# Second attention products issued for two steps at once, and the last tile's chunks transposed by TensorE

## The reference, cut to what matters

```python
# layer 0
x = _layernorm(x + _L0_attn_ref(x, ...))   # 16 heads of 64, every query against all 4096 keys
x = _layernorm(x + _L0_ffn_ref(x, ...))    # rows quantized in blocks of 32, then x @ W.T
# layer 1
x = _layernorm(x + _L1_attn_ref(x, ...))   # 16 query heads, 2 key heads, a window of 256
x = _layernorm(x + _L1_ffn_ref(x, ...))    # sigmoid(xr Wr) * (relu(xk Wk)^2 Wv)

# the first attention
scores = jnp.einsum('bhts,bshd->bhts', q_, k_) * scale + const
attn = jax.nn.softmax(scores, axis=-1)
out = jnp.einsum('bhts,bshd->bthd', attn, v_).reshape(B, T, D)
return quat_linear(out, oW, ob)
```

## Time and profile before

| | us |
|---|---|
| time, median of 3 runs | 2162.46 (2153.24 to 2162.77) |
| the profiled execution | 2166.97 |
| span of its slowest core (3) | 2165.4 |
| spans of the 8 cores | 2133.8 to 2165.4 |
| busy in the span: PE, ACT, DVE, POOL | 1953.6, 1595.8, 1063.2, 406.3 |

### The profile page before, as it was taken

One profiled execution on the slowest core, in us unless ns is written; L12 is line 12 of the kernel. 1 busy time (PEld: TensorE's weight loads), 2 busy tenths in 40 slices (PEclk: granted clock), 3 DMA queues, 4 the chain that ended last, 5 costly groups with the idle time before them and its releaser, 6 DMA issues.

```text
span 2165.4 us, 42335 instructions; the slowest of 8 cores (2133.8 to 2165.4 us)
## 1 busy us (share of the span) xinstructions
PE 1953.6 (90%) x14234; PEld 783.8 (36%) x14234; DVE 1063.2 (49%) x1569; ACT 1595.8 (74%) x2177; POOL 406.3 (19%) x271
## 2 busy tenths in 40 slices
PE   5999998988999999899999999998790899999996
PEld 2444445322222222222222222222440356556653
DVE  6566542575321345423445224453680467777773
ACT  1343348999899999899999999998220577777772
POOL 3000000000010000100001000001010166776665
PEclk9999999999999999999999999999995999999998
DMA  6332311003210010010101104004219211111110
GB/s 98 78 64 54 49 33 46 26 23 92 73 59 6 4 45 26 27 57 6 42 21 33 59 1 90 16 16 117 68 41 112 60 31 41 41 41 50 40 41 40
DMA packets 63855, 100.99 MB, mean 47 GB/s; under 512 B 25617, under 2 KB 46225, under 8 KB 62242
## 3 DMA queue, kind: packets, MB, share of 16 engines
q1 hardware_dynamic: 41138, 67.77, 11.3%
q0 software_dynamic: 22512, 30.51, 8.4%
HBM read 88.86 MB, written 22.02 MB: 51 GB/s over the span
## 4 chain that ended last, share of the span: by engine, by line
PE 57%; ACT 22%; issue 9%; DVE 6%; DMA 4%; POOL 1%; ACTq 1%; DVEq 0%; POOLq 0%; SPq 0%
ACT TE L728 20%; PE PALL L1121 12%; PE PALL L1244 8%; PE PALL L1134 7%; PE PALL L1148 7%; PE PALL L1152 5%; PE PALL L1169 4%; PE PALL L1311 3%; PE PALL L1210 2%; PE PALL L1266 2%; PE PALL L1255 2%; DMA TY<-Y2SP 2%; PE PALL L1257 2%; PE PALL L1276 1%; DMA Y2SP<-TY 1%
## 5 line engine op out<-in xcount | busy, mean ns | idle before, releaser
L728 ACT ACTIVATE TE<-PALL,BIASB 128x1024 bf16<-128x1024 f32 x1088 | 1124.9, 1132 | 85.8 <-PE PALL L1134 76.4
L1134 PE MATMUL PALL<-TE,TY 64*128 64x512 bf16 (+1 forms) x2560 | 429.6, 353 | 73.6 <-ACT TE L728 48.3
L1148 PE MATMUL PALL<-TE,TY 128*64 128x512 bf16 (+1 forms) x2560 | 447.9, 373 | 0.4 <-ACT TE L728 0.4
L1152 PE MATMUL PALL<-TE,TY 128*64 128x512 bf16 x2176 | 423.9, 386 | 0.0
L1134 PEld LDWEIGHTS PALL<-TE,TY 64*128 64x128 bf16 x2560 | 131.4, 93 | 524.6 <-issue 522.5
L1148 PEld LDWEIGHTS PALL<-TE,TY 128*64 128x64 bf16 x2560 | 133.3, 110 | 236.4 <-issue 225.7
L994 DVE COPY TY<-PALL 128x512 f32<-128x512 f32 (+1 forms) x40 | 24.5, 612 | 358.2 <-PE PALL L1152 358.2
L743 ACT ACTIVATE TY<-PALL,SMALL 128x384 bf16<-128x384 f32 x272 | 156.9, 589 | 34.3 <-DVE SMALL L1029 32.4
L600 POOL TENSOR_TENSOR TX<-TX 128x1024 f32<-128x1024 f32 x17 | 40.0, 2354 | 724.2 <-DVE TY L924 724.2
L689 ACT ACTIVATE TX<-PALL,BIASB 128x512 f32<-128x512 f32 (+1 forms) x104 | 66.4, 661 | 141.9 <-PE PALL L1121 141.7
L1029 DVE TENSOR_REDUCE SMALL<-PALL 128x2 f32<-128x768 f32 x136 | 129.7, 954 | 76.1 <-PE PALL L1257 72.9
(11 more groups left out here) (130 smaller groups left out, 2296.4 us busy)
## 6 DMA issues: line engine op xcount, KB each, us to landing
TE<-WOD SPq DMA_DIRECT2D x5, 2048.0 KB, 8.4
TX<-XST SPq DMA_DIRECT2D x17, 512.0 KB, 4.6
TY<-Y2SP POOLq DMA_DIRECT2D x17, 512.0 KB, 3.5
YOUT<-TY SPq DMA_DIRECT2D x17, 512.0 KB, 2.6
TE<-FWD SPq DMA_DIRECT2D x4, 2048.0 KB, 8.3
Y2SP<-TY SPq DMA_DIRECT2D x17, 256.0 KB, 2.2
TE<-XF POOLq DMA_DIRECT2D x8, 512.0 KB, 11.9
TY<-XF POOLq DMA_DIRECT2D x8, 512.0 KB, 10.9
```

Source lines behind the costliest of these rows:

```text
L728: s.activation(EXPS(m), PB(2 * (m % 2), 0, 1024), AF.Exp, bias=BIASB[:, 63:64], scale=0.125).then_inc(*up("exp", m))
L1134: op = t.matmul(PB(2 * (m % 2) + hh, x * w, w), KB(c, (s * k + x) * 128, 128, 64 * hh, 64), QB(c, 0, w, 64 * hh, 64), start=True, stop=Tru ...
L1148: t.matmul(PB(6, 0, w)[64 * hh:64 * hh + 64, :], VB(s * k + x, (2 * c + hh) * 64, 64), EXPS(m)[:, hh * 512 + x * w:hh * 512 + x * w + w], ...
L1152: op = t.matmul(PB(7, 0, 512)[64 * hh:64 * hh + 64, :], ONEB, EXPS(m)[:, hh * 512:hh * 512 + 512], start=(s == 0), stop=(s == SPP[T] - 1), ...
```

## The change

**Attention.** `pv_plan` is gone. At every odd step `n` from 3 on TensorE issues `scores(n)` and then the second products of steps `n - 3` and `n - 2` together: first all products with values of both steps, then all with ones. The first of a group waits for the copy out of bank 6 (`pvn`) only, and the products with ones for that of bank 7 (`pvf`). Nothing is put off at a group's start. The pieces beside are moved to even steps: `o` every second step, `f` at b + 16, 18, 22, 24, 28, 30, 34, 36; `t`, `z2`, `n2` and the load of the next input move by two to five steps.

**Chunks.** `n2` of tiles 0 to 3 writes into `XD` and no longer into `XDT`. `tev` does not wait for the store any more; `n2` waits for the transposes of the next chunk, `quant` for the store of the chunk two before, and `xld` for the store instead of for `n2`.

**Passage.** The four chunks of the last tile are placed anew: the small tile's projections first, `z1` of all four before the first `quant`, `tev` on ScalarE. The last transposed DMA is gone: for each of the four chunks TensorE transposes the chunk (`yt`), ScalarE copies it into `X2` (`yte`), and the ten projections of the chunk follow with 128 columns. The load `wk` is issued right after the attention's last product, the third transposed DMA after the load of `f`'s weights instead of ahead of it.

```diff
-def pv_plan():
-
-
-    plan, due, last = {}, [], 0
-    for m, (T, c, s) in enumerate(STEPS):
-        last = max(last, m + (4 if s == 0 and m else 2))
-        due.append(last)
-    for m, n in enumerate(due):
-        plan.setdefault(n, []).append(m)
...
-            put("pe", o + d * i, "o", T, j, i)
+            put("pe", o + 2 * i, "o", T, j, i)
...
-        put("pe", b + 10, "t", T, j)
-        put("dve", b + 11, "tev", T, j)
-        for i in range(8):
-            put("pe", b + 13 + d2 * i, "f", T, j, i)
-        z = b + 13 + 7 * d2 + 2
-        put("dve", z, "z2", T, j)
-        put("act", z + 4, "r2", T, j)
-        put("dve", z + 6, "n2", T, j)
-        put("sp", z + 6, "y2", T, j)
+        put("pe", b + 12, "t", T, j)
+        put("dve", b + 13, "tev", T, j)
+        for i, f in enumerate((16, 18, 22, 24, 28, 30, 34, 36)):
+            put("pe", b + f, "f", T, j, i)
+        put("dve", b + 38, "z2", T, j)
+        put("act", b + 42, "r2", T, j)
+        put("dve", b + 45, "n2", T, j)
+        put("sp", b + 45, "y2", T, j)
...
-            chunk(T - 1, j, B + (11, 30, 50, 76)[j], B + (27, 46, 71, 92)[j], B + 108 + 32 * j, 2, 3)
-            put("sp", B + 154 + 32 * j, "xld", T, j)
+            chunk(T - 1, j, B + (12, 30, 50, 76)[j], B + (28, 46, 71, 92)[j], B + 108 + 32 * j)
+            put("sp", B + 156 + 32 * j, "xld", T, j)
...
-    put("sp", E, "x2", 2)
-    put("sp", E + 2, "wld", L, "f")
-    put("pool", E + 30, "w1o")
-    put("pool", E + 90, "wr")
-
-    def prep(i, e, d):
-        for oc in range(10):
-            put("pe", e + d * oc, "pre", i, oc)
-            put("dve" if oc == 1 else "act", e + d * oc + 0.5, "prev", i, oc)
-
-    def last(j, o, n1, q, t, z2, n2):
+    put("sp", E, "wld", L, "f")
+    put("sp", E + 1, "x2", 2)
+    put("pool", E + 1, "wk")
+    put("pool", E + 24, "w1o")
+    put("pool", E + 75, "wr")
...
-    last(0, E + 0, E + 10, E + 12, E + 25, E + 36.2, E + 51)
-    last(1, E + 5, E + 25.2, E + 27, E + 38.5, E + 52.5, E + 65.2)
-    last(2, E + 18, E + 37.5, E + 42, E + 53, E + 65.5, E + 70.2)
-    last(3, E + 24.7, E + 52, E + 56.3, E + 66.5, E + 71, E + 75)
-    prep(4, E + 7.5, 1.0)
-    prep(0, E + 19.5, 1.75)
-    prep(1, E + 37.2, 1.75)
-    prep(2, E + 55, 1.75)
-    put("sp", E + 76, "x2", 3)
-    prep(3, E + 82, 1.75)
+    last(0, E + 5, E + 8.6, E + 15.2, E + 24.2, E + 42.4, E + 54)
+    last(1, E + 9, E + 12.2, E + 19.2, E + 33.8, E + 55, E + 66.6)
+    last(2, E + 14, E + 16.2, E + 23.2, E + 45.4, E + 67.6, E + 70.6)
+    last(3, E + 18, E + 20.2, E + 32.8, E + 58, E + 71.6, E + 76)
+    prep((4, -1), [E + 0.5 * n for n in range(10)])
+    prep((0, -1), [E + e for e in (13.5, 17.5, 21.7, 23.5, 25.3, 27, 28.8, 30.6, 32.4, 38)])
+    prep((1, -1), [E + 40 + 2.1 * n for n in range(10)])
+    prep((2, -1), [E + 62.1 + 1.8 * n for n in range(10)])
+    for j in range(4):
+        e = E + 80 + 5 * j
+        put("pe", e, "yt", L, j)
+        put("act", e + 0.4, "yte", L, j)
+        prep((3, j), [e + 0.5 + 0.45 * n for n in range(10)])
...
-            return XDT if T < NT - 1 else bview(TY2, 51200 + 2048 * j, 1024)
+
+            return XD if T < NT - 1 else bview(TY2, 51200 + 2048 * j, 1024)
+
+        def TEV(T):
+
+            return "teva" if T == NT - 1 else "tev"
...
-        PREP = [(i, oc) for i in (4, 0, 1, 2, 3) for oc in range(10)]
+
+
+        PREP = [(i, -1, oc) for i in (4, 0, 1, 2) for oc in range(10)]
+        for j in range(4):
+            PREP += [(NT - 1, j, "yt")] + [(3, j, oc) for oc in range(10)]
...
-                            y.wait_ge(*at("n2", T - 1, j))
+                            y.wait_ge(*at("y2sp", T - 1, j))
...
+                    elif name == "wk":
+                        g.wait_ge(*at("pv", NST - 1))
+                        g.wait_ge(*at("xb", NT - 1, 3))
+                        weight(WKB, WKT, "wk")
...
+                    if name == "tev":
+                        s.wait_ge(*at("tmm", T, j))
+                        s.wait_ge(*at("fmm", *prev_chunk(T, j), 1))
+                        s.activation(XDT, PB(4, 0, 1024, BF16), AF.Copy).then_inc(*up("teva", T, j))
+                        continue
+                    if name == "yte":
+                        s.wait_ge(*at("yt", T, j))
+                        s.activation(bview(TY3, 24576 + 8192 * 3, 4096).rearrange("p (c n) -> p c n", n=512)
+                                     [:, :, 128 * j:128 * j + 128],
+                                     PB(pbank[(T, j, "yt")], 0, 1024, BF16).rearrange("p (c n) -> p c n", n=128),
+                                     AF.Copy).then_inc(*up("yte", T, j))
...
-                    s.wait_ge(*at("pv", m - RING))
+                    s.wait_ge(*at("pv", (m - RING) | 1))
...
+                if T != "w" and (T and j == 0 or T < NT - 1 and j > 1):
+                    v.wait_ge(*at("y2sp", *((T, j - 2) if j else prev_chunk(T, j))))
...
-                                v.wait_ge(*(at("y2sp", *p) if p[0] < NT - 1 else at("fmm", *p, 1)))
+                                v.wait_ge(*at("fmm", *p, 1))
...
+                        if T < NT - 1 and j + 1 < TILES[T][1] // 128:
+                            v.wait_ge(*at("tmm", T, j + 1))
+                        elif T < NT - 1 and j:
+                            v.wait_ge(*at("y2sp", T, j - 1))
...
             def pv(m):
+
                 T, c, s = STEPS[m]
                 w = TILES[T][1]
                 k = 512 // w
-                t.wait_ge(*at("exp", m))
-                if s == 0 and m:
+                first, last = s == 0, s + 1 == SPP[T] - 1
+                t.wait_ge(*at("exp", m + 1))
+                if first and m:
+                    t.wait_ge(*at("pvn", T if c else T - 1, (c - 1) % 8))
+                for d in (0, 1):
+                    for x in range(k):
+                        for hh in (0, 1):
+                            t.matmul(PB(6, 0, w)[64 * hh:64 * hh + 64, :],
+                                     VB((s + d) * k + x, (2 * c + hh) * 64, 64),
+                                     EXPS(m + d)[:, hh * 512 + x * w:hh * 512 + x * w + w],
+                                     start=(first and d == 0 and x == 0), stop=(last and d == 1 and x == k - 1),
+                                     tile_position=(0, 64 * hh))
+                if first and m:
                     t.wait_ge(*at("pvf", T if c else T - 1, (c - 1) % 8))
-                for x in range(k):
-                    first, last = s == 0 and x == 0, s == SPP[T] - 1 and x == k - 1
+                for d in (0, 1):
                     for hh in (0, 1):
-                        t.matmul(PB(6, 0, w)[64 * hh:64 * hh + 64, :], VB(s * k + x, (2 * c + hh) * 64, 64),
-                                 EXPS(m)[:, hh * 512 + x * w:hh * 512 + x * w + w],
-                                 start=first, stop=last, tile_position=(0, 64 * hh))
-                for hh in (0, 1):
-                    op = t.matmul(PB(7, 0, 512)[64 * hh:64 * hh + 64, :], ONEB, EXPS(m)[:, hh * 512:hh * 512 + 512],
-                                  start=(s == 0), stop=(s == SPP[T] - 1), tile_position=(0, 64 * hh))
-                op.then_inc(*up("pv", m))
+                        op = t.matmul(PB(7, 0, 512)[64 * hh:64 * hh + 64, :], ONEB,
+                                      EXPS(m + d)[:, hh * 512:hh * 512 + 512], start=(first and d == 0),
+                                      stop=(last and d == 1), tile_position=(0, 64 * hh))
+                op.then_inc(*up("pv", m + 1))
...
+                    elif name == "yt":
+                        n = PREP.index((T, j, "yt"))
+                        t.wait_ge(*at("n2", T, j))
+                        t.wait_ge(*at(*readout(PREP[n - 4])))
+                        for c in range(8):
+                            op = t.transpose(PB(pbank[PREP[n]], c * 128, 128, BF16), Y2O(T, j)[:, c * 128:c * 128 + 128],
+                                             IDB)
+                        op.then_inc(*up("yt", T, j))
...
-                for m in PV.get(n, ()):
-                    pv(m)
+                if n % 2 and 3 <= n < NST + 2:
+                    pv(n - 3)
...
```

116 lines of the change are left out of this document (63 added, 53 removed).

## The result

The changed kernel takes 2073.65 us in the median of four runs (2066.16 to 2130.69), the kernel before 2161.75: a ratio of 0.959, with a 95% interval of 0.954 to 0.963. In some executions of every kernel here the cores of a die show a lower clock and the time is longer (2130.69 is one); the ratios, and the medians given with the experiments, go without them. The profiled execution took 2080.28 us. So I take 2067 as the kernel's time and read core 3, the slowest of the other six. First the spans and clocks of the cores.

The account below looks back on a forecast made before the run. Attention bound by ScalarE in plain steps (1.00 us) and TensorE beside pieces (1.15), passage by its chain of waits. 2165.4 - 21 - 4 - 8 - 53 = 2079, plus 1.6 is 2081, less 1 is 2080; range 2065 to 2095.

Parts of the forecast that it names:

- The rule for a pause: Attention: scores over 1.20 us after the previous ones stop ScalarE for the excess; 0.13 us per plain pair.
- the sum's 10 us for the small activations: Attention: normalizations' small activations push exponentials back; 3 us a tile in tiles 2 to 4, 1 in tile 1.
- its 0.54: Attention: ScalarE's loss at each of 39 group starts with three second products in a row, 21 us, saved by the change.
- VectorE late at group starts: Rival, attention: bank 7 copied too late, margin 0.13 us; 0.5 lost at each start, total 2100; chance 0.15.
- No pause in plain pairs: Rival, attention: 315 pairs without a piece stay at 2.00 us, 41 less, total 2039; chance 0.10.
- Part 2: Attention chunks: copy no longer waits for the previous chunk's store; nothing added to the sum; only a 20 us store shows.
- Part 3, the start: Passage up to chunk 3's transposes near 1601: small projections, output products, then VectorE's four quantisations, 42.5 us, about 10 between.
- they lie in the 5.97 and cost nothing: Passage start: the small tile's ten projections, 4.3 us, fit TensorE's 5.97 us wait for the attention's last division.
- Part 3, the end: Passage from 1601: TensorE's remaining 16 us, then four chunks at 6.2 each, 24.8, to 1642; layer 1 starts 1.1 later.
- the slow `n2`: Passage: allowance of 2 us for VectorE's slow normalisation (2.86), making the passage 125 us, -53.
- The transposed load: Third transposed DMA, started with `wk` at the attention's end: 41.31 us, needed some 75 us on, so hidden, 34 to spare.
- Layer 1 unchanged: Layer 1 was to last 467 us, as before (466.9).

Follow-up runs that it names:

- The run that repaired it: Changed kernel with five of the small tile's ten projections issued behind the first output products instead of ahead of them: ratio 0.957, passage 134.1 us.

## Why the prediction was right, and where not

- **The time**: 2080 against 2073.65, with the range holding it. Part of this is luck, for two errors offset each other: 23 too dear in the attention, 12.5 too cheap in the passage, and 4 for layer 1. Against 2067 the forecast is 13 too high, and still in its range.
- **The rule for a pause**: right that a pair's gap of 1.31 outruns the buffers, right in 2.17 for a pair with a piece, wrong in "a gap of g costs g - 1.2 whenever g is over 1.2". From an exponential to the scores that take its buffer, over the pair to the next scores and on to their exponential lie 1.26 + 1.31 + 0.55 = 3.12 us, and three pitches. I took two of them as free of pauses and put the whole 0.12 into each pair. But those three pitches contain the pause of two neighbouring pairs: 1.11 + 1.01 + 1.00 is enough. So it is 0.06 a pair, 315 x 0.07 = 22 us less than the sum had, nearly the attention's whole error. The rest nearly cancels: the sum's 10 us for the small activations have no place of their own after, while pairs with a piece take 2.18 in the mean on core 3 and those with transposes 2.40, where the sum has 2.17 for both. The run with one more product bears the rule out (2 x 0.11 for 0.216 more of gap in two plain pairs), and the run with plain pairs issued singly shows that the pause is the pair's. In the earlier trace rows the rule was tested on a single gap far from others, where it holds; it failed where gaps recur.
- **Where the attention's gain comes from**: of the 45 us by the medians, 36 are the pairing (the run without it) and the rest is the store and differences in tile 0. Within the pairing, what the pieces gain (27 in tiles 1 to 4) and what plain pairs lose (22) nearly cancel, and the group starts are what remains: 24 to 29 us for 32 of them, 0.76 to 0.90 each where the prediction had 0.54. The prediction took its 0.54 from a start without a piece; with a piece behind the three products ScalarE stood 0.96.
- **VectorE late at group starts** (chance 0.15): did not happen; the margin of 0.13 was enough. **No pause in plain pairs** (0.10): half true, 2.06 lies midway between its 2.00 and 2.13.
- **Part 2**: the store's wait is gone, worth 3 to 6 us in the old places; but in the new places the buffer was not needed: the later `f` covers the wait, as the run with the old buffer shows.
- **Part 3, the start**: "they lie in the 5.97 and cost nothing" failed on the value piece, whose readout stands behind the division: the first output products came 12.7 behind the last exponential, where they came 7.9 behind it before (1519.29 to the 1527.22 of the earlier trace rows). The run that repaired it showed that this is not what was late next: the quantisation behind all four chunks began 33.4 behind the last exponential's start where the sum has 28.7 (1548 less 1519.29), and between the four quantisations lay 15 us and not "about 10" (57.8 to the last transposes in place of 53). That is 9.5 of the 12.5. (The expectation of the run with the early quantisation puts the two at 27.7 and 52.5, which makes 11.) The term was mis-sized because I summed VectorE's busy time and left out what it waits for, in the order in which its queue stands: it is busy for 31.8 of the 47.0 us up to its second quantisation.
- **Part 3, the end**: 16 for the rest of tile 2 was exact (1556.68 to 1572.66). From there to layer 1 core 3 took 31.4, where the sum has 24.8 and 1.1, and 2 for the slow `n2`. A chunk took 6.45 in place of 6.2 (1590.24 to the next at 1596.69), but the second one took 10.78, with the pause of 2.55, one of 1.38 behind it, and a clock of 0.63 and 0.51 in the two windows of 2 us after that (1584 to 1588). The other five cores of the six don't have this and take 133.8 to 135.5 for the passage, not 138.6.
- **The transposed load**: right that it is hidden (28.5 us on core 3, and no one waits). The prediction does see that its 41.31 stand beside a weight load, but it does not ask what the load would take alone, 7.8. The weight load beside it was the price, and moving it gives 28 of the passage's 38 us, which the prediction does not say.
- **Layer 1 unchanged**: wrong by 4 us. They come with the early weight load (462 with that edit alone). Which wait in layer 1 they were I did not trace.

## What to carry to other kernels

A gap that outruns double buffering costs its excess once over the stretch that the chain over the buffers spans, and neighbouring gaps whose pauses fall into one such stretch share it: write the chain out over several periods before a price is put on it. Before a slow transfer is replaced, look at what shares the DMA engines with it: moving one 2 MB load gave 28 of the 38 us that the rebuilt passage gave. And on an engine that runs in order, a queue's length is its busy time and its waits in the order of the program; taking one wait away shows only the next one.

## What was not expected of the hardware

- A transposed load of 512 rows took 7.8 us with no weight load beside it and 41.3 beside a 2 MB load, on other cores 23 to 41 beside the same load; even with the weights for `f` and `wk` beside it, at the attention's end, it took 28.5.
- The cores of one kernel differ by up to 17 us in the attention when second products go step by step with three at a group's start (1193 to 1210), and by 1.5 when they go in pairs (1153.0 to 1154.5). Part of it is tile 0, 68 to 76 us from core to core where the clock dips. Another part is the store: TensorE's waits behind it are 1.1 to 7.0 us a core, and without tile 0 the two slowest cores (1134, the others 1125 to 1127) are among the three that wait over 6. The group starts differ as well, 24 to 29 us over pairs in the run without the pairing. Why they do was not traced.
- In the chain of small products of the last chunks TensorE now and then stands for "issue": 2.55 us in the middle of eight transposes above, on some cores and in some executions only (the run with the output products first has none on the same core, and 0.35 to 1.75 on four others). What it waits for no row says.
